# A state-space layer's channel statistics gathered by ScalarE, and its second norm's steps in another order

## The reference, cut to what matters

```python
def _L1_conv_ref(x, ...):                        # x already group-normed
    u = x.reshape(Bsz, C, H * W).transpose(0, 2, 1)
    fx = _layernorm(u, ln1_g, ln1_b)             # first norm
    res = fx
    ...
    Bu = jnp.einsum('ph,blh->blp', B_bar, fx)    # complex, 192 states
    _, xs = jax.lax.associative_scan(binop, (lam_el, Bu), axis=1)
    y = 2.0 * jnp.real(jnp.einsum('hp,blp->blh', Cc, xs)) + D * fx
    y = jax.nn.gelu(y, approximate=False) + res
    fy = _layernorm(y, ln2_g, ln2_b)             # second norm
    z1, z2 = jnp.split(fy @ W_enc.T, 2, axis=-1)
    y = (z1 * jax.nn.gelu(z2, approximate=False)) @ W_dec.T + fy
    return y.transpose(0, 2, 1).reshape(Bsz, C, H, W)

# _gn(v): mean and variance over 12 channels x 32 x 32 of each of 32 groups
x = x + _L1_conv_ref(_gn(x), ...)
```

## Time and profile before

| what | value |
|---|---|
| median of 3 runs | 4251.5 us (4245.55 to 4254.65) |
| the profiled execution | 4248.17 us, its span 4246.4 us |
| PE busy | 3846.9 us (91%) |
| DVE busy | 3092.6 us (73%) |
| ACT busy | 2300.1 us (54%) |
| POOL busy | 1402.0 us (33%) |

### The profile page before, as it was taken

One profiled execution on the slowest core, in us unless ns is written; L12 is line 12 of the kernel. 1 busy time (PEld: TensorE's weight loads), 2 busy tenths in 40 slices (PEclk: granted clock), 3 DMA queues, 4 the chain that ended last, 5 costly groups with the idle time before them and its releaser, 6 DMA issues. The chain is left out here.

```text
span 4246.4 us, 54195 instructions
## 1 busy us (share of the span) xinstructions
PE 3846.9 (91%) x17373; PEld 2366.5 (56%) x17373; DVE 3092.6 (73%) x3183; ACT 2300.1 (54%) x3658; POOL 1402.0 (33%) x1142
## 2 busy tenths in 40 slices
PE   6999999999999999955899999465999999999999
PEld 5776868686867677722455555244444444444444
DVE  4767666676767675647989886356878888888878
ACT  1867767685858585834443442223544644644644
POOL 1857667575748485831211100221000000000000
PEclk8999999999999999977999999688999999999999
DMA  3333324242324332220121112775011010010010
GB/s 118 85 93 93 102 82 112 74 116 78 102 84 106 89 95 79 59 79 32 38 80 55 50 45 62 198 220 187 0 45 43 2 44 33 11 44 25 20 44 15
DMA packets 117836, 312.13 MB, mean 74 GB/s; under 512 B 48146, under 2 KB 49762, under 8 KB 108914
## 3 DMA queue, kind: packets, MB, share of 16 engines
q1 hardware_dynamic: 105650, 264.17, 20.7%
q0 software_dynamic: 10960, 37.38, 3.9%
q10 hardware_dynamic: 1008, 7.67, 0.5%
HBM read 203.12 MB, written 101.30 MB: 72 GB/s over the span
## 5 line engine op out<-in xcount | busy, mean ns | idle before, releaser
L417 POOL TENSOR_TENSOR probs_lo<-probs,probs_hi 128x512 fp32r<-128x512 f32 x848 | 1169.2, 1394 | 641.7 <-ACT probs L463 620.8
L530 DVE TENSOR_REDUCE maxima<-m_psum 128x1 fp32r<-128x1024 f32 x512 | 625.1, 1222 | 368.1 <-PE m_psum L706 367.4
L462 ACT ACTIVATE probs_hi<-s_psum 128x512 fp32r<-128x512 f32 x1024 | 613.3, 599 | 383.5 <-PE o_psum L735 221.8
L2510 PE MATMUL psum<-mixes,last_weights 128*128 128x512 f32 x1728 | 751.1, 592 | 0.0
L463 ACT ACTIVATE probs<-s_psum 128x512 f32<-128x512 f32 x1024 | 609.0, 595 | 0.0
L2510 PEld LDWEIGHTS psum<-mixes,last_weights 128*128 128x128 f32 x1728 | 327.5, 190 | 409.8 <-issue 409.8
L719 PE MATMUL s_psum<-q_all,k_hi 128*128 128x512 f32 x1024 | 430.8, 421 | 25.9 <-ACT probs L463 25.6
L735 PE MATMUL o_psum<-probs_lo,v 128*112 128x512 f32 x1024 | 412.1, 402 | 12.7 <-DVE probs_lo L610 6.5
L730 PE MATMUL o_psum<-probs_hi,v 128*112 128x512 f32 x1024 | 404.4, 395 | 0.0
L720 PE MATMUL s_psum<-q_all,k_lo 128*128 128x512 f32 x1024 | 404.3, 395 | 0.0
L2517 PE MATMUL psum<-xp,last_weights 128*128 128x512 f32 x864 | 381.9, 596 | 18.3 <-DVEq L2394 13.3
(11 more groups left out here) (338 smaller groups left out, 6240.3 us busy)
## 6 DMA issues: line engine op xcount, KB each, us to landing
xin<-x SPq DMA_DIRECT2D x17, 1536.0 KB, 6.8
xin<-in_x SPq DMA_DIRECT2D x16, 1536.0 KB, 7.3
k_hi<-k_rows_hi SPq DMA_DIRECT2D x128, 192.0 KB, 3.4
k_rows_hi<-stage_hi SPq DMA_DIRECT2D x48, 256.0 KB, 2.1
k_rows_lo<-stage_lo SPq DMA_DIRECT2D x48, 256.0 KB, 2.3
q_rows_hi<-stage_hi SPq DMA_DIRECT2D x48, 256.0 KB, 2.2
q_rows_lo<-stage_lo SPq DMA_DIRECT2D x48, 256.0 KB, 2.6
k_lo<-k_rows_lo SPq DMA_DIRECT2D x64, 192.0 KB, 4.4
```

The lines of the kernel that those rows point to most:

```text
L417: pool.tensor_tensor(probs_lo[:, u % RING, :], probs[:, u % RING, :], as_f32(probs_hi[:, u % RING, :]), ALU.subtract).then_inc(pool_low.ne ...
L462: nc.scalar.activation(probs_hi[:, u % RING, :], s_psum[:, u % 2, :], ACT.Exp, scale=SCALE)
L530: nc.vector.tensor_reduce(maxima[:, g % 2, tile:tile + 1], source, AX.X, ALU.max, negate=True).then_inc(rows_max.next(), 1)
L2510: ins = nc.tensor.matmul(bank, conv_w[:, t, down, factor, m * P:(m + 1) * P], mixes[:, factor, t, down:down + S, :].rearrange("p a b -> p ...
```

## The change

- The input's statistics of batch i + 3 are no longer bn_stats on DVE but sums and sums of squares on ACT (`input_sums`: six activations of 128 x 1024 with an accumulated output, behind the last gate). The three prologue inputs stay on DVE (`early_moments`).
- The output's statistics likewise: `output_sums(i, 0)` (two activations of 128 x 1536) between the second and third Gelu of the next y, `output_sums(i - 1, 1)` between the second and the third gate of turn i. DVE only reduces three or two columns (`moments`, `out_moments`); `out_moments(i - 1)` stands between the second `apply_gate` and the first norm's `scale`.
- ACT takes the second norm's inverses ahead of the first norm's squares, and writes both halves of the whole y (`wholes(i, 0)` between the two halves of `highs`); DVE's first half goes.
- DVE: in `turn_in` of the second half the four products come ahead of the first norm's `centre` (`behind_products`); two of the late outputs of batch i - 1 come ahead of `lows(i, 0)`. In turn -2, where `turn_in` isn't run, `centre` now comes behind `table(1)`.
- PE: the first two encoder banks (`fill_enc(i, 0, 1)`) come ahead of the column means of the first norm's squares.
- ACT's third gate comes ahead of `affine`.

```diff
 # PE, turn i
                 if batch(i - 1):
                     fill_dec(i - 1, EARLY, 2 * CT)
+                if here:
+                    fill_enc(i, 0, 1)
                 if third:
                     sums(norm1, norm_psums[0], first_sums[:, 0, :], summed_sq1, varied1, i + 2)
                 if here:
-                    fill_enc(i)
+                    fill_enc(i, 1, 2 * CT)
 # in fill_enc the wait for y_hi is now tile by tile
-                    if m == 0:
-                        pe.wait_ge(high_made.sem, high_made.at(CT * (half + 1), i))
+                            if m == 0 and k == 0:
+                                pe.wait_ge(high_made.sem, high_made.at(CT * half + t + 1, i))
 # ACT, turn i
+                if batch(i):
+                    inverses(norm2, varied2, inv_made2, i)
                 if batch(i + 2):
                     squares(norm1, first_sums, f1[i % 2], centred1, squared1, i + 2)
                 if batch(i):
-                    inverses(norm2, varied2, inv_made2, i)
-                    highs(i)
+                    highs(i, 0)
+                    wholes(i, 0)
+                    highs(i, 1)
                 if batch(i + 2):
                     inverses(norm1, varied1, inv_made1, i + 2)
                 if batch(i):
                     gates(i, 0, 1)
-                    wholes(i)
+                    wholes(i, 1)
                     gates(i, 1, 2)
+                if batch(i - 1):
+                    output_sums(i - 1, 1)
+                if batch(i):
+                    gates(i, 2, 3)
                 if batch(i + 2):
                     affine(f1[i % 2], rows["ln1_g"], rows["ln1_b"], scaled1, f1_made, i + 2)
...
                 if batch(i):
-                    gates(i, 2, 2 * CT)
+                    gates(i, 3, 2 * CT)
+                if batch(i) and batch(i + 3):
+                    input_sums(i + 3)
...
+            def output_sums(i, half):
+                act.wait_ge(out_made.sem, out_made.at(CT * (half + 1), i))
+                for kind in range(2):
+                    if x_summed.count:
+                        act.wait_ge(x_summed.sem, x_summed.now())
+                    if out_summed.count:
+                        act.wait_ge(out_summed.sem, out_summed.now())
+                    nc.scalar.activation(first_sums[:, :, cols(half)], residuals[i % 2][:, :, cols(half)], (ACT.Identity, ACT.Square)[kind],
+                                         accum_out=out_sums[:, kind, half:half + 1]).then_inc(out_summed.next(), 1)
 # DVE, turn i
-                if third:
-                    centre(norm1, f1[i % 2], averaged1, centred1, i + 2)
+                def centre_first():
+                    if third:
+                        centre(norm1, f1[i % 2], averaged1, centred1, i + 2)
+
+                def scale_second():
+                    if here:
+                        scale(norm2, y, inv_made2, scaled2, i)
+                    if batch(i - 1):
+                        outputs(i - 1, EARLY, 2 * CT - 1)
+                    if here:
+                        lows(i, 0)
+
                 if i == -2:
                     table(1)
...
                 if after:
-                    turn_in(i + 1, 1, scale_second)
-                elif here:
+                    turn_in(i + 1, 1, centre_first, scale_second)
+                else:
+                    centre_first()
                     scale_second()
                 if batch(i - 1):
-                    outputs(i - 1, EARLY, 2 * CT)
+                    outputs(i - 1, 2 * CT - 1, 2 * CT)
...
+                if batch(i - 1):
+                    out_moments(i - 1)
                 if third:
                     scale(norm1, f1[i % 2], inv_made1, scaled1, i + 2)
 # in lows(i, 0): DVE's own whole y goes
-                    for t in range(CT):
-                        nc.vector.tensor_scalar(whole[:, t, cols(0)], y[:, t, cols(0)], rows["ln2_g"][:, t:t + 1], rows["ln2_b"][:, t:t + 1],
-                                                ALU.mult, ALU.add).then_inc(f_first_half.next(), 1)
```

More of the change, by code:

```diff
@@ L1220, in affine, with highs, wholes @@
                                              scale=g[:, t:t + 1], bias=b[:, t:t + 1]).then_inc(made.next(), 1)
-            def highs(i):
+            def highs(i, half):
                 if i > 0:
                     act.wait_ge(hidden.sem, hidden.at(4 * CT, i - 1))
-                for half in range(2):
-                    act.wait_ge(scaled2.sem, scaled2.at(half + 1, i))
-                    for t in range(CT):
[L1228 to L1232, removed]
+                act.wait_ge(scaled2.sem, scaled2.at(half + 1, i))
+                for t in range(CT):
+                    nc.scalar.activation(y_hi[:, t, cols(half)], y[:, t, cols(half)], ACT.Identity,
+                                         scale=rows["ln2_g"][:, t:t + 1], bias=rows["ln2_b"][:, t:t + 1]).then_inc(high_made.next(), 1)
+            def wholes(i, half):
+                if i >= 2 and half == 0:
                     act.wait_ge(stored, 16 * (i - 1))
@@ L1235, in wholes, with input_sums @@
                 for t in range(CT):
[L1236 to L1237 removed]
+                    nc.scalar.activation(residuals[i % 2][:, t, cols(half)], y[:, t, cols(half)], ACT.Identity,
+                                         scale=rows["ln2_g"][:, t:t + 1], bias=rows["ln2_b"][:, t:t + 1]).then_inc(f_made.next(), 1)
+            def input_sums(i):
+                act.wait_ge(x_loaded, 16 * (i + 1))
+                for n in range(2 * CT):
+                    t, kind = n // 2, n % 2
+                    if n >= 2:
+                        act.wait_ge(x_summed.sem, x_summed.now() - 1)
+                    nc.scalar.activation(first_sums[:, 1 + kind, :], xin[:, t * T:(t + 1) * T], (ACT.Identity, ACT.Square)[kind],
+                                         accum_out=x_sums[:, kind, t:t + 1]).then_inc(x_summed.next(), 1)
+            def output_sums(i, half):
[7 more added lines that the diff above has]
+                                         accum_out=out_sums[:, kind, half:half + 1]).then_inc(out_summed.next(), 1)
             def swap(source, half, made):
@@ L1293, in _, with early_moments, out_moments @@
                         nc.scalar.activation(at, at, ACT.Gelu).then_inc(y_gelu.next(), 1)
+                        if n == 1 and batch(i):
+                            output_sums(i, 0)
+                elif batch(i):
+                    output_sums(i, 0)
+                    output_sums(i, 1)
         @block.vector
         def _(dve):
[L1297 to L1300, removed]
+            def early_moments(i):
+                dve.wait_ge(x_loaded, 16 * (i + 1))
+                gn.vector_moments(dve, xin[:, :], step, None, gn_moments)
             def moments(i):
-                gn.vector_total(dve, 2 * CT, step, None, gn_moments)
+                dve.wait_ge(x_summed.sem, 2 * CT * (i - 2))
+                nc.vector.tensor_reduce(gn.both[:, :], x_sums[:, :, :], AX.X, ALU.add).then_inc(step.next(), 1)
+                dve.wait_ge(step.sem, step.now())
+                nc.vector.tensor_scalar(gn.both[:, :], gn.both[:, :], 1.0 / (CT * T), None, ALU.mult).then_inc(gn_moments.next(), 1)
+            def out_moments(i):
+                out = moments_out[:, i, :]
+                dve.wait_ge(out_summed.sem, out_summed.at(4, i))
+                nc.vector.tensor_reduce(out, out_sums[:, :, :], AX.X, ALU.add).then_inc(step.next(), 1)
+                dve.wait_ge(step.sem, step.now())
+                nc.vector.tensor_scalar(out, out, 1.0 / (CT * T), None, ALU.mult).then_inc(out_measured.next(), 1)
             def group_shift(i):
@@ L1428, in outputs @@
                 xres = residuals[i % 2]
[L1429 to L1445, removed]
-                dve.sem_inc(gn.turn, 1)
-                nc.vector.bn_aggr(out, out_stats[:, :, :].rearrange("p a b -> p (a b)")).then_inc(step.next(), 1)
-                dve.wait_ge(step.sem, step.now())
-                nc.vector.scalar_tensor_tensor(out[:, 1:2], out[:, 0:1], out[:, 0:1], out[:, 1:2], ALU.mult, ALU.add).then_inc(out_measured.next(), 1)
+                for n in range(first, end):
+                    m, half = n % CT, n // CT
+                    if n == 0:
+                        dve.wait_ge(res_added, 16 * CT * (i + 1))
+                    dve.wait_ge(decoded.sem, decoded.at(n + 1, i))
+                    nc.vector.tensor_tensor(xres[:, m, cols(half)], xres[:, m, cols(half)], bank("dec", i, n), ALU.add).then_inc(out_made.next(), 1)
             def add_tiles(tile, half, summed, first, i):
```

41 lines of the change are left out of this document (15 added, 26 removed).

## The result

The changed kernel takes 4271.4 us in the median of 5 runs (4265.87 to 4275.82), the kernel before, beside it on the same chip, 4252.1 (4245.55 to 4254.76): ratio 1.0047 [1.0032, 1.0061], slower by 0.5%. Forecast were 4266 in a range of 4238 to 4277, and slower as the likeliest. The profiled run took 4265.87 with a span of 4264.1, against 4246.4 before: +17.7.

What follows compares the result with a forecast made beforehand. TensorE and VectorE are nearly full, and VectorE makes projection c late. Middle turns +12.0, batch 0 +3, batch 6 -1.2 and prologue +1.0 sum to +14.8 us: 4263 on the profiled 4248.2, 4266 for the median, range 4238 to 4277.

Steps and rivals of the forecast that it cites:

- Late gate: Likeliest case: column means behind two encoder banks hold ScalarE's inverses and the first gate; slower, 4266 us, chance 0.50.
- Steps 5 and 7: First gate waits for the later means, starting 57.4 us into the period; half clock in encoder adds 1.2 us.
- step 2: First norm's scaling on VectorE: POOL's adds beside it lengthen it by 0.5 us (0 to 1.2).
- the 57 to 60 given as a sign: Sign in the new trace: the first gate starts between 57 and 60 us into the period.
- Steps 1, 3, 4 and 6: Decoder stall goes; scaling at 41.6, lows at 47.8; second encoder bank's 1.90 wait goes; gate to c 27.9 to 28.0.
- Step 7: TensorE's encoder bank and means run at half clock after a longer, emptier stretch: 1.2 us more (0 to 1.9).
- Batch 0's turn: The turn of batch 0 has the new gate wait and no late outputs to gain from: +3 us (1.5 to 5).
- Late gate, nothing else lost: Rival: first gate late, but clock stays up or returns early and POOL costs no more: +4.8, 4256; chance 0.25.
- Square's table: Rival: Square on ScalarE needs another table, so two loads stand around the output sums between gates: 4272; chance 0.02.
- VectorE's load decides: Rival: encoder's first bank ends earlier, means don't hold the gate; faster, at most 28 us, half-way 4238; chance 0.23.
- the floor of 79.7: TensorE's period without its three stalls and the half-clock encoder bank, 5.7 us in all: some 79.7 us.

Runs made afterwards that it cites:

- Means first: The changed kernel with the column means of the first norm's squares ahead of the first two encoder banks again: 4249.5 us, ratio to before 1.0002.
- POOL late: The changed kernel with POOL's second-half sums of squares held back until VectorE's lows are made: 4259.7 us, ratio to before 1.0029.
- norms back: The changed kernel with means ahead of the encoder, first-norm squares ahead of second-norm inverses, and centre ahead of the products again: 4231.1 us, ratio to before 0.9959.
- statistics only: The kernel before with only the statistics moved, sums on ScalarE and VectorE's bn_stats gone, the rest in the old order: 4250.4 us, ratio 1.0004.
- all together: "norms back" with the prologue's centre ahead of table(1) and out_moments behind the last turn_out: 4225.6 us, ratio to before 0.9951.
- order only: The changed kernel's order with all statistics back on VectorE as bn_stats: 4265.9 us, ratio to before 1.0037.

## Why the prediction was right, and where its sizes were off

**Late gate: right.** In the shown turn the slow projection sets everything back by 17.41 - 15.72 = 1.69 us; less that, the means end at t = 56.1, the gate starts at 59.3 and VectorE takes it at 59.9. Steps 5 and 7 with step 2 gave 57.4 + 0.5 + 1.2 = 59.1 for its start. As it stands in the trace the gate starts at t = 61.0, outside the 57 to 60 given as a sign, because of the slow projection. "Means first" shows the cause: it moves the means alone, and the whole loss goes.

**Steps 1, 3, 4 and 6: right.** The decoder runs in one piece, the scaling starts at t = 41.5 (41.6), the lows at 47.6 (47.8), the second bank waits for nothing. From the gate's product to c are 27.27 us, where 27.9 to 28.0 were forecast: the waits of out_moments and of the fourth gate came out at 0.46 and 0.43, for 1.0 and 0.5.

**Step 2: right mechanism, other place.** The scaling still takes 4.97, so nothing is added there. POOL's adds reach into the lows, which take 2.96 instead of 1.88: +1.1, where I took 0.5. "POOL late" brings the 1.88 back. The Trainium skill, "SBUF — State Buffer", section "Who interferes with whom", lets the second comer wait for all of the first. The trace agrees, in size too: beside the lows runs one add, which takes 1.72 us there and 1.26 in the prologue, where VectorE has only bn_stats beside it, and the lows grew by 1.08. That is nearer to the 1.3 us that the prediction took from this rule than to its own 0.5. POOL's timeline of the changed kernel, in the prologue and beside the lows:

```profile
1916.04 1.26 POOL L1184 TENSOR_TENSOR first_sums<-first_sums 128x512 f32<-128x512 f32 x1
...
2299.03 1.72 POOL L1184 TENSOR_TENSOR first_sums<-first_sums 128x512 f32<-128x512 f32 x1
```

**Step 7: right.** The second bank takes 2305.54 - 2302.54 = 3.00, +0.94 at granted clock 0.50; taken were 1.2. In one turn, from 2427.34, bank and means are both slow and the turn is 90.38.

**The missing term.** The forecast of a middle turn was +2.4; the shown one has +3.5, and the five together +17.5 instead of +12.0. What is missing is the clock at c, a term that the prediction put at nothing. Its own numbers held it: means ending at 54.2, then ten banks at 2.06 and a decoder of 7.9 bring TensorE to c at 82.7, and c was put at 86.1, a wait of 3.4 where there had been 1.00. I never asked what that wait would do, although show a clock that falls behind one of 1.90. Measured is a wait of 2.45 and a projection that takes 1.69 us longer, in four of the five turns; without it the shown turn would be 87.19, against the 87.8 forecast, and the one middle turn whose projection ran at full clock did take 87.45.

**The small terms.** Batch 0's turn took +5.5, outside the bound of 5.0 (3 was the value), with the same late gate. Batch 6's took -1.5 (-1.2). The prologue took +1.4 to the first c (1.0), the layer's end -0.3 (0). The layer began 3.9 us earlier in this execution; batch 0's statistics are joined at 1885.0 us in its trace, at 1888.9 in that of before and at 1888.8 in that of "norms back", so this is not the change's doing. The sum is -3.9 + 1.4 + 5.5 + 17.5 - 1.5 - 0.3 = +18.7, and the layers behind it give back 1.0: +17.7. So the layer itself lost 22.6 us, where 14.8 were forecast. That the whole came out nearer is luck, 4.9 us of it outside the layer: the mechanism was right, its size a third too small.

**The rivals.** "Late gate, nothing else lost" falls by the clock of both places and the lows. "Square's table" falls: the sums between the gates run under Gelu's table with no load beside them, as the rows of ScalarE after show (Square is the one at 2315.38), and the reading of the accumulator takes 0.19 us more, where 0.2 was taken. "VectorE's load decides" falls for this order, and "statistics only" shows that the load alone decides nothing. But its bound was about right: with the means early, the turn of "all together" falls to 81.13, of which 0.60 at c and 1.17 in the decoder are waits; that leaves 79.4, near the floor of 79.7 that the prediction worked out.

## What to carry to other kernels

Taking work from a nearly full engine gained nothing here while the waits on its way stayed where they were; follow the one chain to the next hand-over, here means, inverses, gate, and ask what now stands ahead of each link on its in-order queue. When a forecast delays one of two engines, work out how long the other then waits, and whether its clock stays up behind such a wait. A change that loses as a whole can hold a part that wins: here what was left once the means, the squares and centre were back in their old places, the sums on ScalarE, the outputs ahead of the lows and the earlier third gate together.

## What the runs showed of the hardware

- Behind waits at c of up to 1.4 us the projection ran at full clock in all the turns read (15.72 us). Behind waits of 1.88 to 2.47 it went both ways: of the changed kernel's six, four took 17.41 and two 15.72 (behind 1.94 and 2.47); of the six in "order only", all behind 1.88 to 1.95, two took 17.41 and four 15.72. The second encoder bank in "statistics only" did the same behind 1.90. So the wait alone doesn't settle it; what does stays open.
- Keeping the clock up at one place did not add up: with c's wait filled, the encoder's bank behind it took 0.84 us more than without, and the means 0.58.
- An activation with an accumulated output leaves a second record, ACTIVATION_READ_ACCUMULATOR, of 0.19 us; the 1536-column activation itself takes 1.48, as without it.
- Three lows of 512 columns take 1.88 us alone and 2.96 beside one of POOL's adds; table(1)'s ten instructions take 9.5 us in the changed kernel, with no add beside them, where they took 13.3.
